# Where the projection, norm and router of the first three batches stand: each in the attention batch after its own, or all in the last one

## The reference, cut to what matters

```python
def _L1_attn_ref(query, kv_k, kv_v, Wq, Wo):        # 16 heads of 16, 4096 keys
    Q = (query @ Wq.T).reshape(B, QL, HEADS, HEAD_DIM)
    scores = jnp.einsum('bqhd,khd->bhqk', Q, K) * SCALE
    attn = jax.nn.softmax(scores, axis=-1)
    out = jnp.einsum('bhqk,khd->bqhd', attn, V).reshape(B, QL, HIDDEN)
    return out @ Wo.T
...
def _L1_ffn_ref(x, gate_w, ..., shgate_w, ...):
    logits = jnp.einsum('td,ed->te', xf, gate_w)
    ...
    sgate = jax.nn.sigmoid(xf @ shgate_w)[:, None]
...
x = x + _L1_attn_ref(_layernorm(x), ...)
x = x + _L1_ffn_ref(_layernorm(x), ...)
```

## Time and profile before

| | |
|---|---|
| median of 3 runs | 2264.12 us (2259.59 to 2273.28) |
| the profiled execution's own time | 2266.55 us |
| its span (first to last instruction on the core) | 2264.8 us |
| mean granted PE clock | 0.931 of full |
| busy | PE 2026.0, DVE 1572.4, ACT 1360.1, POOL 261.8 us |

### The profile page before, as it was taken

The page is one execution under the profiler, slowest core; times in us unless marked ns, Lnnn a source line. Parts: engine busy times, 40 slices in busy tenths (PEclk is TensorE's granted clock), DMA queues, the critical chain, the costliest instruction groups (busy, mean ns, idle before and its releaser), DMA issues. The chain is left out here.

```text
span 2264.8 us, 40076 instructions
## 1 busy us (share of the span) xinstructions
PE 2026.0 (89%) x15956; PEld 1067.1 (47%) x15956; DVE 1572.4 (69%) x1951; ACT 1360.1 (60%) x2700; POOL 261.8 (12%) x274
## 2 busy tenths in 40 slices
PE   6793999991578999999999999999999999999884
PEld 3552889991223343343343334334334333536663
DVE  3337112215598999998999999999999998215334
ACT  1220444440116888887888888888888888653221
POOL 0001334431020000000000000000000000002462
PEclk9795999995567999999999999999999999979997
DMA  4201668755716000006000005000020000001124
GB/s 138 88 4 65 213 224 258 257 179 139 102 44 69 13 2 13 13 1 69 13 2 13 13 13 57 13 13 1 13 79 2 2 2 2 20 21 25 58 82 153
DMA packets 150034, 140.93 MB, mean 62 GB/s; under 512 B 75506, under 2 KB 122590, under 8 KB 149086
## 3 DMA queue, kind: packets, MB, share of 16 engines
q1 hardware_dynamic: 140446, 112.72, 21.1%
q0 software_dynamic: 9408, 25.70, 3.6%
HBM read 106.40 MB, written 31.72 MB: 61 GB/s over the span
## 5 line engine op out<-in xcount | busy, mean ns | idle before, releaser
L1003 DVE TENSOR_REDUCE maxp<-banks 128x2 f32<-128x1024 f32 x1024 | 1238.8, 1224 | 68.2 <-PE banks L997 61.9
L1435 ACT ACTIVATE pring<-banks 128x512 f32<-128x512 f32 x2048 | 1109.2, 595 | 244.3 <-PE banks L1316 168.2
L1330 PE MATMUL banks<-pring,vcur 128*17 128x256 f32 x8192 | 650.5, 390 | 9.4 <-ACT osb L1429 7.3
L997 PE MATMUL banks<-kst,qst 48*128 48x512 f32 x2048 | 527.5, 513 | 38.4 <-DVE maxp L1003 26.1
L1316 PE MATMUL banks<-qst,kst 50*128 50x512 f32 x2048 | 432.0, 410 | 0.0
L997 PEld LDWEIGHTS banks<-kst,qst 48*128 48x128 f32 x2048 | 196.0, 188 | 474.2 <-issue 344.6
L1330 PEld LDWEIGHTS banks<-pring,vcur 128*17 128x17 f32 x8192 | 136.9, 95 | 325.9 <-issue 182.5
L1316 PEld LDWEIGHTS banks<-qst,kst 50*128 50x128 f32 x2048 | 264.9, 187 | 35.0 <-issue 17.7
L766 ACT ACTIVATE hT<-banks,b 128x128 f32<-128x128 f32 x295 | 108.2, 368 | 186.7 <-PE banks L703 171.1
L904 DVE TENSOR_SCALAR yo<-banks,wblock 128x256 f32<-128x256 f32 x59 | 28.5, 483 | 223.8 <-PE banks L712 223.8
L1301 POOL TENSOR_TENSOR acc<-xn,orec 128x256 f32<-128x256 f32 x15 | 9.3, 621 | 1259.9 <-DVE orec L1480 1259.9
(11 more groups left out here) (304 smaller groups left out, 1312.6 us busy)
## 6 DMA issues: line engine op xcount, KB each, us to landing
w1r<-in_L_ffn_w SPq DMA_DIRECT2D x59, 640.0 KB
kst<-key_parts SPq DMA_DIRECT2D x24, 512.0 KB, 17.7
key_parts<-ksp SPq DMA_DIRECT2D x32, 256.0 KB
w2all<-in_L_ffn_w SPq DMA_DIRECT2D x12, 640.0 KB, 7.7
w2all<-expert_rows SPq DMA_DIRECT2D x12, 512.0 KB, 8.2
qst<-query_parts SPq DMA_DIRECT2D x96, 64.0 KB, 2.3
normed_rows<-xn SPq DMA_DIRECT2D x8, 512.0 KB, 2.9
kf<-in_kT SPq DMA_DIRECT2D x16, 256.0 KB
```

Of the source, the lines that this page charges most:

```text
L997: mm = nc.tensor.matmul(ps[:, base + r, :], qst[i][rows, hp, qt * P:(qt + 1) * P], keys[rows, hp, kb * 512:(kb + 1) * 512], start=True, st ...
L1003: return nc.vector.tensor_reduce(maxp[:, B % 2, :, hp, qt, kb], ps[:, base:base + 2, :], X, ALU.max)
L1330: mm = nc.tensor.matmul(ps[32 * j:32 * j + VC, 7, cols], vcur[g % 2][:, kt, j, :], pring[:, (G % 2) * HG + j, cols], start=(kt == 0 and ha ...
L1435: nc.scalar.activation(pring[:, n % (2 * HG), :], ps[:, n % 3, :], ACT.Exp, scale=float(DH) ** -0.5).then_inc(exp_done, 1)
```

## The change

The table `FRONTS` (three lists of key tiles, all in batch 15) becomes one list `FRONT`, used for each of sequences 0, 1 and 2 in its own batch: sequence b in batch 13 + b. Waits and the places of the store and of the power operation follow. Seven front units thus stand in batch 13, seven in batch 14 and seven in batch 15.

```diff
-            FRONTS = [[0, 1, 3, 4, 7, 8, 10], [5, 6, 9, 11, 14, 15, 17], [13, 16, 18, 19, 22, 23, 26]]
+            FRONT = [7, 9, 12, 15, 19, 21, 24]
...
-                for b, kts in enumerate(FRONTS):
-                    for n, kt in enumerate(kts):
-                        plan[(BATCHES - 1) * NKT + kt].append(("front", b, n))
+                for b in range(NB - 1):
+                    for n, kt in enumerate(FRONT):
+                        plan[(BATCHES - NB + b + 1) * NKT + kt].append(("front", b, n))
...
 # SP
+                        if g == NG - 1 and i:
+                            store_rows(sp, i - 1, NB)
+                            sp.wait_ge(rows1_out, 16 * i)
                         if B + 1 < BATCHES:
                             sp.wait_ge(rows_ready, B + 2)
                             load_maxima(sp, (B + 1) % NB)
...
-                    for b in range(NB - 1):
-                        store_rows(sp, b, NB)
-                        sp.wait_ge(rows1_out, 16 * (b + 1))
...
 # POOL
                     for B in range(BATCHES - 1):
+                        if B > BATCHES - NB:
+                            norm_pool(pool, B - BATCHES + 2 * NB - 1, main)
                         pool.wait_ge(outs_ready, B + 1)
...
-                    for b in range(NB - 1):
-                        norm_pool(pool, NB + b, main)
+                    norm_pool(pool, 2 * NB - 2, main)
...
 # ACT, turn_out
+                                if i > BATCHES - NB:
+                                    act.wait_ge(rows1_out, 16 * (i - BATCHES + NB))
...
 # DVE, front_results, n = 3
-                                if b:
-                                    dve.wait_ge(rows1_out, 16 * b)
-                                else:
-                                    dve.wait_ge(out_done, BATCHES - 1)
+                                dve.wait_ge(out_done, BATCHES - NB + b + 1)
```

## The result

The changed kernel takes 2297.78 us (median of 4 runs, 2292.06 to 2299.91) against 2263.05 for the kernel before (4 runs). The ratio is 1.0138, 95% interval 1.0118 to 1.0159: the change makes the kernel slower, by 31 us if the ratio is applied to the time of before (the medians are 34.7 us apart). The spans of the profiled executions, 2295.9 and 2264.8 us, are 31.1 apart.

What follows compares the result with a forecast made beforehand. DVE and PE were taken to have no room in an ordinary batch, PE and ACT to pace batch 15. Cost 2 x (18.0 + 2.9) = 41.8 less gain 16.3 gave +25.5 us, 2292.1 profiled, 2290 predicted; range 2266 to 2310.

Steps and rivals of the forecast that it cites:

- What bounds the kernel: Ordinary batch: a half-step costs 1.22 us on PE and 1.23 on DVE, neither has room; PE and ACT pace batch 15.
- the reading of weight-load busy time: Ordinary batch: weight loads busy 32.64 of 82.00 us would give PE much room; fronts cost DVE's own time alone; weighed, not followed.
- The price at full clock: Batches 13 and 14: DVE time lost to one front without clock falls, 18.0 us per batch, lower bound 9.0.
- transposes: Three transpose units without the extra wait, batches 13 and 14: DVE's next reduction comes 0.96 us later each, 2.9 together.
- first product: First product with Wo, batches 13 and 14: waits for the reduction of the max unit just ahead; cost 3.5 us.
- product with norm: Second product, no wait, then the norm of 4.45 us without reductions, batches 13 and 14; cost 6.1 us.
- transposes behind the wait: Transposes held by the reduction of the max unit just ahead, batches 13 and 14; cost 2.1 us.
- The waits at n = 2, 4, 6: PE held ahead of first product, one transpose unit and router; without this each batch costs some 3.5 us less.
- one fall of 2.9 us in each: Batches 13 and 14: PE's pause of 3.2 us at the norm brings one fall to half clock, 2.9 us per batch.
- The upper bound given, 23.8 per batch: Batches 13 and 14: 18.0 us plus 5.8 for two falls, the second behind the wait at the router; 47.6 for both.
- a fall behind the router at tile 24: Batch 15: half clock over the seven tiles after the router, 8.8 us, leaving a gain of 16.3 instead of 25.1.
- Rival 2: Batch 15: clock falls early, in tiles 0 to 6, until the first product at tile 12; 15 us more, 2305; chance 0.15.

Runs made afterwards that it cites:

- Experiment 3: Changed kernel with the products with Wo of sequences 0 and 1 done twice on PE in batches 13 and 14; 2306.40 us.
- experiment 1: Changed kernel, but PE waits for the front unit on which its unit depends, not the unit just ahead in the list; 2290.82 us.
- experiment 4: Changed kernel, but the norm is split: DVE scales the rows at tile 17, not right behind the statistics in tile 15; 2298.32 us.
- experiment 6: Kernel before, with all three router units in tile 31, the last of batch 15; 2258.23 us.
- experiment 2: Changed kernel, but the routers of sequences 0 and 1 stand in batch 15 (tiles 3 and 5); 2284.09 us.
- experiment 5: Kernel before, with only sequence 2's router moved, from tile 26 to tile 31 of batch 15; 2256.49 us.
- experiment 8: Kernel before, with only sequence 0's front moved to batch 13; sequences 1 and 2 stay in batch 15 at their old places; 2282.13 us.
- experiment 7: Changed kernel with PE waiting for its own front unit, the norm split in two, and all routers in tile 31 of batch 15; 2268.34 us.

## Why the prediction was right, point by point

**What bounds the kernel: right.** DVE and PE both run an ordinary batch without room. Experiment 3 shows it for PE, by work that only PE has, and experiment 1 too: with the wait gone DVE still idles 0.96 us ahead of the first product. The trace does not agree with the reading of weight-load busy time that the prediction weighed: batch 13 of the changed kernel has PE's weight loads busy for 40.74 of 108.40 us, and yet more PE work costs nine tenths of its length.

**The price at full clock: right in its parts.** Foretold against read off DVE's timeline after: transposes 0.96 against 1.1 each; first product 3.5 against 3.6; product with norm 6.1 against 6.1; transposes behind the wait 2.1 against 2.2 (at full clock, batch 14). The router has no instance at full clock after the change; with its foretold 3.4 the sum is 18.6 us against 18.0. The waits at n = 2, 4, 6, put at 3.5 us per batch: experiment 1 took 1.19 us from DVE's wait at the first of them, so 3.6 for three.

**The clock in batches 13 and 14: the mechanism was right, the size was not.** I took one fall of 2.9 us in each. In the changed kernel each batch has 23.9 us at half clock, in three stretches and in two. What the batches grew by, 26.9 and 26.7, less 18.6, leaves 8.3 and 8.1 us for it. I had counted the norm's pause alone as a trigger in the forecast, and the router only as an upper bound, though both falls of the kernel before stood behind routers. The upper bound given, 23.8 per batch, was passed by 3 us, and so were the 100 to 105 us foretold for the length of these batches (108.4 and 107.2). A pause of 3 us was rightly taken for a trigger. But the contrast that stood beside it, a pause of 1.86 us without a fall, is not a property of that pause: the wait at the start of batch 7, 1.45 to 1.86 us in the ten profiles, has a fall within 2 us in four of them (changed kernel, experiments 1, 4 and 6).

**The clock in batch 15: wrong the other way.** I took a fall behind the router at tile 24 that would cost 8.8 us; in the profiled execution none came, and the batch gained 23.6 us instead of 16.3 (without a fall 25.1 was forecast). Most of the 1.5 us between are two small things: tiles without a unit take 2.16 to 2.23 us there, where I took the 2.17 of one tile, and PE waits once for 0.56 us for ACT's copy of the sums. Rival 2, an early fall, did not occur. That is shown for the tiles without units: they kept 1.00 after the change and in experiment 6.

**The sum.** These two errors nearly cancelled: +10.6 in batches 13 and 14, -7.3 in batch 15, +1.2 for the parts of the price, and 1 us outside. +25.5 was foretold and 31.1 measured in the spans. The range and the direction held; that the time came out so near is partly luck, the more so as the profile of the changed kernel has falls in batches 4 and 7 and that of before only in batch 4.

**Where the clock falls.** Eight profiles (before, after, experiments 1 to 5 and 8) hold 24 router units apart from one another, and 31 falls of the clock in batches 13 to 15. 18 of them begin during a router unit or at most 2 us behind its end, 9 at a norm pause of 3.0 us, in it or within 2 us (all nine such pauses have one), and 4 at the transposes of tile 19 that wait for a reduction. No fall begins anywhere else in these batches. Each count is of one execution per kernel. Pauses of PE alone don't explain it: 11 of the 18 falls at routers had no pause ahead of the router. The other seven routers, in batches 13 and 14, had waited 1.1 us, and all seven have a fall; without that wait it is 11 of 17. What follows a short pause seems to matter: nine pauses of 1.15 us ahead of the first product had no fall, and of eight of 1.0 to 1.5 us ahead of the transposes four had one. Moving the routers away removes theirs (experiments 2, 6, 7) and shortening the pause removes those at the norm (4, 7). Why 6 of the 24 routers had none, and how long a stretch lasts (3.4 to 27 us beside max units), stays open, and so does what it is in a router that brings the fall.

## What to carry to other kernels

Before work is moved out of the longest stretch, ask what paces the stretch that receives it: here a front costs 6 us without and 8 with its router in a batch where DVE is free, and 10 (waits mended, without the router) to 19 at full clock in one where DVE has no gap, so the shorter batches were the dearer place. A wait written as "the unit just ahead" changes its meaning when the order changes; write it for the unit on which the work depends. Where a kind of work is seen to be followed by half clock, as the router here, it belongs at the end of a stage, where the slower clock has the least left to slow.

## What the runs showed of the hardware

A unit of 16 matmuls with nine columns each, itself without idle time of PE, has a fall to half clock in it or within 2 us in 18 of 24 cases, and in 11 of the 17 that had no pause ahead of them either. Tiles of scores and values without any unit held 2.4 GHz for as long as they ran. The state sticks: once at 1.2 GHz, the same tiles stayed there for 29.1 us to the end of batch 15 (experiment 4) with PE marked busy for 28.86 of them. A pause of 3.0 us brought a fall nine times out of nine. A wait of 1.45 to 1.86 us at one and the same place brought one in four executions of ten, so that a single trace without a fall does not show a pause to be harmless.
